# A perceiver block on one core: the tail after the cross attention, done batch by batch inside the loops

## The reference

```
x = x + xattn(layernorm(x), ctx, ctx)      # 16 heads, 2048 keys per batch
x = x + attn(layernorm(x))                 # 16 "heads" by a plain reshape, + its own layernorm
x = x + ffn(layernorm(x))                  # router argmax over 4 experts

# attn: Q = x@wq+bq ; K, V alike ; reshape(B*16, 128, 32) ; softmax(QK^T/sqrt(32)) V ; reshape back ; @wo + bo + x ; layernorm
# ffn:  logits = x @ W_router ; e = argmax(logits)
#       h = gelu(x @ W1[e] + b1[e])        # W1: 4 experts of 512 x 2048
#       y = layernorm(h @ Wo + bo + x)
```

## Time and profile before

| | us |
|---|---|
| median of 3 runs | 601.75 (601.21 to 604.71) |
| the profiled execution | 603.38 |
| its span, first to last instruction | 601.6 |
| PE busy | 528.6 (88%) |
| PE weight loads | 393.9 (65%) |
| DVE busy | 311.2 (52%) |
| ACT busy | 184.1 (31%) |
| POOL busy | 37.2 (6%) |
| mean granted TensorE clock | 0.933 of full |

### The profile page before, as it was taken

The page is one execution under the profiler, slowest core; times in us unless marked ns, Lnnn a source line. Parts: engine busy times, 40 slices in busy tenths (PEclk is TensorE's granted clock), DMA queues, the critical chain, the costliest instruction groups (busy, mean ns, idle before and its releaser), DMA issues.

```text
span 601.6 us, 8656 instructions
## 1 busy us (share of the span) xinstructions
PE 528.6 (88%) x3550; PEld 393.9 (65%) x3550; DVE 311.2 (52%) x561; ACT 184.1 (31%) x282; POOL 37.2 (6%) x32
## 2 busy tenths in 40 slices
PE   6999999999989899999999587934555999999995
PEld 5777767777767688777767455823225788888642
DVE  4545335566756411175757222874286579766122
ACT  3110053737363431136363720493222000000400
POOL 0300000003940000000000000000000000000000
PEclk9999999999989999999999798977765699999999
DMA  8600000004300000300004420000020565542000
GB/s 290 253 0 1 1 1 1 2 2 144 138 0 3 1 0 1 139 3 2 1 1 185 167 99 9 0 3 1 0 70 2 244 246 200 212 173 113 0 8 28
DMA packets 7998, 41.24 MB, mean 69 GB/s; under 512 B 1172, under 2 KB 2196, under 8 KB 4116
## 3 DMA queue, kind: packets, MB, share of 16 engines
q1 hardware_dynamic: 7960, 40.69, 18.3%
HBM read 40.16 MB, written 0.52 MB: 68 GB/s over the span
## 4 chain that ended last, share of the span: by engine, by line
PE 80%; DVE 9%; ACT 5%; issue 3%; DMA 1%; POOL 0%; SPq 0%; POOLq 0%; DVEq 0%; ACTq 0%
PE ps L778 41%; PE ps L835 10%; PE ps L821 6%; PE ps L1051 5%; PE ps L1052 5%; PE ps L1053 5%; PE ps L850 5%; ACT VT L396 2%; DMA wv_raw<-in_xWv 1%; PE ps L1040 1%; DVE rden L665 1%; DVE Pm L526 1%; DVE small L484 1%; DVE cT L672 1%; ACT Pm L325 1%
## 5 line engine op out<-in xcount | busy, mean ns | idle before, releaser
L333 ACT COPY PT<-ps 128x512 f32<-128x512 f32 x96 | 53.3, 588 | 102.0 <-PE ps L835 102.0
L835 PE MATMUL ps<-ident,Pm 128*128 128x128 f32 x512 | 71.1, 282 | 4.9 <-ACT PT L333 2.7
L835 PEld LDWEIGHTS ps<-ident,Pm 128*128 128x128 f32 x512 | 57.8, 143 | 24.9 <-issue 16.9
L526 DVE TENSOR_SCALAR_CACHE_REDUCE Pm<-ps,small 128x512 f32<-128x512 f32 x96 | 66.4, 748 | 8.6 <-PE ps L821 8.6
L325 ACT ACTIVATE Pm<-Pm,small 128x2048 f32<-128x2048 f32 x32 | 64.2, 2006 | 14.2 <-DVE Pm L526 14.2
L778 PE MATMUL ps<-ctxH,wkH 128*128 128x512 f32 x124 | 52.0, 419 | 2.8 <-DVE Kr L506 2.4
L1051 PE MATMUL ps<-w1H,zH 128*128 128x512 f32 x128 | 50.7, 396 | 0.0
L778 PE MATMUL ps<-wvH,ctxH 128*128 128x512 f32 x128 | 50.3, 393 | 0.2 <-DVE wvL L570 0.2
L1052 PE MATMUL ps<-w1L,zH 128*128 128x512 f32 x128 | 50.5, 395 | 0.0
L1053 PE MATMUL ps<-w1H,zL 128*128 128x512 f32 x128 | 50.3, 393 | 0.0
L778 PE MATMUL ps<-wvL,ctxH 128*128 128x512 f32 x128 | 50.0, 391 | 0.0
(11 more groups left out here) (151 smaller groups left out, 718.4 us busy)
## 6 DMA issues: line engine op xcount, KB each, us to landing
w1raw<-in_W SPq DMA_DIRECT2D x16, 1024.0 KB, 4.8
raw<-in_ctxT SPq DMA_DIRECT2D x7, 1024.0 KB, 4.9
woF<-in_ffn_Wo SPq DMA_DIRECT2D x1, 4096.0 KB, 14.0
rows<-in_rows SPq DMA_DIRECT2D x6, 256.0 KB, 3.9
raw<-in_ctxT SPq DMA_DIRECT2D x2, 512.0 KB, 6.2
wv_raw<-in_xWv SPq DMA_DIRECT2D x2, 512.0 KB, 8.5
wq<-in_xWq SPq DMA_DIRECT2D x1, 1024.0 KB, 12.9
wo<-in_xWo SPq DMA_DIRECT2D x1, 1024.0 KB, 4.7
```

What stands on the lines that cost most here:

```text
L333: act.copy(PT[:, c % 2, i, :, :].rearrange("p k t -> p (k t)"), ps[:, T_BANKS[i % 2], :]).then_inc(pt_act, 1)
L526: dve.tensor_scalar(Pm[:, i, c * CH:(c + 1) * CH], ps[:, i, :], -1.0, mx[:, p % 2, i, c - 1:c] if c else NOT_YET, ALU.mult, ALU.min, accum ...
L835: last = pe.transpose(ps[:, T_BANKS[i % 2], j * P:(j + 1) * P], Pm[:, i, c * CH + j * P:c * CH + (j + 1) * P], ident[:])
```

## The change

The tail is written for one batch at a time.

- **Batch 0's second attention** is placed among the 16 blocks of value products at the end of round 4: the cross attention's output product, layernorm, transposes, Q, K, V, scores, softmax, transposes and outputs, each step after one or two blocks. Its Q, K and V products have 128 moving columns in place of 256. DVE and ACT get its steps between the copies of V blocks. The four weights of this stretch come one after the other through one buffer `wS`, each loaded when the product before it is done.
- **Batch 0's steps up to the router and the masked tokens** are placed in rounds 5 to 8 (`alongside` on DVE; `attention2_out`, `normalized_T`, `logits`, `masks` on PE). They use PSUM bank 6, which is also the bank of the keys, so `keys` waits for them at two places (`u_done`, `x2T_done`), and all the cross attention's other banks stay as they were.
- **Batch 0's experts** are plain fp32 products of the raw W1 tiles (`first_experts`, 4 matmuls for a tile, no split), through a ring of four raw buffers; two tiles in round 8, the others between the steps of batch 1's chain, which runs after round 8 as the whole tail did before.
- **Batch 1's experts** are as before, in fp32r with split tiles, but the 16 tiles of W1 are loaded a second time, and the high part is made on ACT (L525), the low part on DVE (L916). Batch 0's gelu, transposes and the first two quarters of its output product are placed between tiles 1 and 2, after 7 and after 11.
- The biases of the experts are one plain fp32 matmul for each chunk instead of two in fp32r. The addition of the cross attention's output bias to x moves from round 7 to round 1.

The core of the diff, with lines left out:

```diff
             for p in range(1, NP + 1):
                 more = p < NP
                 late = p >= 2 and p != G + 1
+                if p == NP:
+                    onehots_T(0)
+                    first_experts(0)
                 if more:
+                    if p == G + 2:
+                        pe.wait_ge(u_done, 1)
+                    if p == G + 3:
+                        pe.wait_ge(x2T_done, 1)
                     keys(p, 0)
...
                 for c in range(C):
+                    if p == G + 1 and c == 3:
+                        attention2_out(0)
+                    if p == G + 2 and c == 3:
+                        normalized_T(0)
+                    if p == G + 3 and c == 3:
+                        masks(0)
                     probs_T(p - 1, c, 0)
                     probs_T(p - 1, c, 1)
                     if c == 0 and more:
                         keys(p, 2)
+                    if c == 0 and p == NP:
+                        first_experts(1)
...
                 if p == G:
                     weighted_values(p - 1, C - 1)
                     reciprocals_T(p - 1)
-                    for c in range(C):
-                        for j in range(JT):
-                            values(1, c, j)
+                    while_values(0)
+                    while_values(1)
+                    attention_out(0)
+                    while_values(2)
+                    while_values(3)
+                    tokens_T(0)
+                    while_values(4)
+                    features(0, 0)
+                    while_values(5)
+                    while_values(6)
+                    features(0, 1)
+                    while_values(7)
+                    while_values(8)
+                    features(0, 2)
+                    while_values(9)
+                    scores2(0)
+                    while_values(10)
+                    while_values(11)
+                    probs2_T(0, 0)
+                    probs2_T(0, 1)
+                    while_values(12)
...
+                    values2_T(0)
+                    while_values(14)
+                    outputs2(0)
+                    while_values(15)
...
+            def first_experts(n):
+                if n == 0:
+                    pe.wait_ge(s_done, NP * C * HPG)
+                pe.wait_ge(z0_done, n // KT + 1)
+                pe.wait_ge(w1_in[n % RING], 16 * (n // RING + 1))
+                for c in range(IC):
+                    last = pe.matmul(ps[:, c, :], z[:, n, :], w1raw[n % RING][:, c * CH:(c + 1) * CH],
+                                     start=(n == 0), stop=False)
+                last.then_inc(first_tile, 1)
...
+            for n in range(NW1):
+                k = NW1 + n
+                act.wait_ge(w1_in[k % RING], 16 * (k // RING + 1))
...
+                if n >= 2:
+                    act.wait_ge(w1_tile, n - 1)
+                act.copy(w1H[n % 2][:], w1raw[k % RING][:]).then_inc(w1_hi, 1)
...
+            for n in range(NW1):
+                dve.wait_ge(w1_hi, n + 1)
...
+                dve.tensor_tensor(w1L[n % 2][:], w1raw[(NW1 + n) % RING][:], w1H[n % 2][:].bitcast(F32),
+                                  ALU.subtract).then_inc(w1_split, 1)
```

More of the change, by code:

```diff
@@ L877, in _ @@
                 pe.wait_ge(norm_done, b + 1)
[L878 removed]
+                transposes([xn[:, b, k * P:(k + 1) * P] for k in range(KT)], b, xT_mm)
             pe.wait_ge(xT_done, B)
@@ new lines, in attention2_out, with normalized_T @@
+            def attention2_out(b):
+                pe.wait_ge(wS_in, 16 * 5)
+                pe.wait_ge(cT_dve[b], HPG * (2 if b else HPG))
+                if b:
+                    pe.wait_ge(cT_act[b], 2 * HPG)
+                else:
+                    pe.wait_ge(k_done, C * (G + 2))
+                product(ps[:, O2_BANKS[b], :], [(cT[b][:, k, :], wS[:, k, :]) for k in range(KT)]).then_inc(o2_mm, 1)
+            def normalized_T(b):
+                pe.wait_ge(norm_done, LN4[b] + 1)
+                if not b:
+                    pe.wait_ge(k_done, C * (G + 3))
+                transposes([y[b][:, k, :] for k in range(KT)], XT_BANKS[b], x2T_mm)
@@ new lines, in logits, with masks @@
+            def logits(b):
+                pe.wait_ge(wr_in, 16)
+                pe.wait_ge(x2T_done, b + 1)
+                if not b:
+                    pe.wait_ge(s_done, (G + 3) * C * HPG)
+                product(ps[:, LOGIT_BANKS[b], 2 * P:2 * P + E], [(yT[b][:, k, :], wr[:, k, :]) for k in range(KT)])\
+                    .then_inc(logit_mm, 1)
+            def masks(b):
+                pe.wait_ge(z_ready, b + 1)
+                if not b:
+                    pe.wait_ge(k_done, C * NP)
+                for e in range(E):
+                    last = pe.matmul(ps[:, MASK_BANKS[b], e * T:(e + 1) * T], onehot[:, b, e:e + 1].to_broadcast([P, P]),
+                                     ident[:], start=True, stop=True)
+                last.then_inc(mask_mm, 1)
@@ new lines, in hidden_T, with ffn_out @@
+            def hidden_T(b, c):
+                pe.wait_ge(gelu_done[b], c + 1)
+                transposes([hid[b][:, (4 * c + k) * P:(4 * c + k + 1) * P] for k in range(KT)], 4 * b + c, hT_mm[b])
+            def ffn_out(b, c):
+                pe.wait_ge(woF_in, 16 * KT)
+                if c == 0 and b:
+                    pe.wait_ge(hT_dve[0], 1)
+                pe.wait_ge(hT_dve[b] if c % 2 else hT_act[b], c // 2 + 1)
+                for k in range(KT * c, KT * (c + 1)):
+                    last = pe.matmul(ps[:, b, :], hidT[b][:, k, :], woF[:, k, :], start=(k == 0), stop=(k == IT - 1))
+                if c == KT - 1:
+                    last.then_inc(f_mm, 1)
@@ new lines, in _ @@
+            logits(1)
+            first_experts(14)
+            masks(1)
+            onehots_T(1)
+            first_experts(15)
+            expert_bias(0)
+            for n in range(NW1):
+                second_experts(n)
+                if n == 1:
+                    for c in range(KT):
+                        hidden_T(0, c)
+                if n in (7, 11):
+                    ffn_out(0, n // KT - 1)
+            expert_bias(1)
+            ffn_out(0, 2)
+            ffn_out(0, 3)
```

957 lines of the change are left out of this document (536 added, 421 removed).

## The result

| | before | after |
|---|---|---|
| median of 4 runs each, us | 602.56 (601.21 to 604.71) | 569.1 (567.0 to 569.39) |
| ratio | | 0.9434, 95% interval 0.9396 to 0.9472 |
| span of the profiled execution, us | 601.6 | 566.8 |
| mean granted clock | 0.933 | 0.975 |

The forecast was 567.0, so it missed by 2.1 us of 33.5.

A forecast was written before the change was run, and what follows sets the result against it. PE was taken as busy nearly throughout except in the tail's first 119 us, where steps wait and the clock is low. 387.7 + 82.6 + 61.0 + 33.4 = 564.7, plus 2 for the clock: span and time 567 us, range 556 to 583.

The forecast's parts named there:

- the low clock's allowance: Ahead of the experts, behind thin bias products: 2 us added to the sum for PE at low clock.
- Step 1: Value products: batch 0's second attention among the blocks makes the stage 65.6 us instead of 43.6, +22.0.
- the walk's narrow margins: Value products: wk and wv land half a microsecond before they are wanted; softmax's fourth piece at 52.3, wanted at 54.
- Step 2: Rounds 5 to 7: added PE work +6.0, a wait for u_done before round 6 +2.7, smaller terms; sum +7.9 us.
- Step 3: Round 8: two of batch 0's expert tiles go in and delay the exponentials; PE goes on 2.8 us later.
- Step 4: Batch 1's chain: batch 0's tiles cover its steps, 80.5 us of PE work plus gaps, 82.6 us instead of 118.4.
- Step 5: Batch 1's experts: a loop of ACT, DVE and PE over two buffer pairs, 3.6 us a tile, 61.0 us in all.
- Step 6: End: biases, output products, transposes and last layernorm take 33.4 us.
- (a): Value products and rounds: in-order queues bite, six steps by some 2 us, 579 us; chance 0.17.
- (b): Batch 1's experts run at the low clock because of 0.9 us holes per tile, 591 us; chance 0.07.
- (c): Behind round 8: W1 is read twice and DMAs set the pace, 664 us; chance 0.03.
- (d): 128-column products cost 0.221 us and batch 1's expert loop 3.3 us a tile, 559 us; chance 0.10.

The follow-up runs named there:

- e5: The changed kernel with three pairs of split buffers instead of two in batch 1's experts; 561.16 us, ratio 0.9306.
- e2: The changed kernel with batch 0's second attention placed behind the 16 value blocks instead of among them; 597.37 us.
- e6: The changed kernel with DVE's addition behind u_done moved ahead of step 5's last four score passes; 564.62 us, ratio 0.938.
- e7: The changed kernel with round 8 reordered: reciprocals' product before the first expert tile, fourth exponential earlier, masked tokens a round later; 564.5 us, ratio 0.9366.
- e1: The changed kernel with batch 0's expert tiles 2 to 15 moved behind batch 1's chain on PE; 611.75 us.
- e3: The changed kernel loading only 64 of 2048 columns of each tile in the second reading of W1, leaving work out; 567.31 us.
- e4: The changed kernel with batch 1's experts in plain fp32 too, without the split; 574.49 us, ratio 0.9536.
- e8: The changed kernel with the edits of e5, e6 and e7 together; 554.53 us, ratio 0.9202.
- e9: The changed kernel, two pairs kept, with batch 1's bias products one group each behind expert tiles 2 to 5; 564.81 us, ratio 0.9369.
- e10: The changed kernel with the edits of e5, e6, e7 and e9 together; 552.14 us, ratio 0.9155.

## Why the prediction was right, step by step

The mechanisms of all six steps were found in the traces. That the sum agrees to 0.1 us in the span (566.7 and 566.8) is luck, for errors cancel: rounds 5 to 7 and round 8 came 5.4 us longer together, and three terms (the value products, the chain, the low clock's allowance) 6.1 shorter. The 2 us for the low clock were put behind the biases, where this execution paid nothing, and none into the rounds, where it paid 5.7; in e5 the rounds paid 1.9 and the end 3.4.

**Step 1, value products: +20.5 for +22.0.** PE has no wait and a clock of 1.00 there, so the walk's narrow margins (wk, wv, the softmax) all held; e2 shows what they hide, 30 us. The term that was off is the 128-column fp32 product, taken at 0.256 us. The chain of waits of the kernel after gives it:

```profile
403.50 10.98 PE ps L942 x96
```

96 records are 48 products, 0.229 us each, near the lower bound of 0.221. "The weight load is what doesn't shrink" was the wrong choice: records stand 0.114 us apart there while each one's weight load is 0.192 us long in the trace, so the loads overlap and don't set the pace. All 96 products in the two chains make 2.6 us less than I had, 1.3 of the 1.5 us in this stage.

**Step 2, rounds 5 to 7: +10.2 for +7.9.** The wait at `u_done` came where it was forecast, 3.4 us against 2.7, and e6 shows both that it is DVE's order that makes it and what was left out: behind it, twelve matmuls at half clock, +2.5 us. These two are 3.2 us more than forecast, so the rest of these rounds came 0.9 below.

**Step 3, round 8: +5.9 for +2.8.** The same omission: a wait of 3.3 us, then a tile at 6.62 us for 3.43. e7 gets 4.9 of the 5.9 back by the order alone, so most of the price was that of the queue's order and the clock, not of the work put there.

**Step 4, batch 1's chain: 80.0 for 82.6.** PE's work of 80.5 us was the bound; 1.3 are again the 128-column products, the gaps came to 1.4 us (80.0 less 78.56 busy), not 2, and the last 0.7 are in the rest of PE's work. e1 shows the cover: without the tiles 69.7 us for the chain, with 30 us of it idle.

**Step 5, batch 1's experts: 61.5 for 61.0.** The mechanism is confirmed by e5: with a third pair 53.3. The parts: the cast measured 1907 ns, which answers to the extrapolated 1.97, the low part 2.29. Casts of the loop start alternately 3.4 and 4.1 us apart, that is 7.5 us for two tiles, where 7.2 was forecast: the hand-overs between engines take 0.5 to 0.6, not 0.2. The Trainium skill ("ScalarE: Activation LUTs", What ACT_TABLE_LOAD costs) had given an estimated 1.89 us for the cast, and the trace agrees with that formula to 1%. The groups of DVE and ACT in the expert stage, kernel after (busy and mean, then idle and who ended it):

```profile
L916 DVE TENSOR_TENSOR w1L<-w1raw,w1H 128x2048 fp32r<-128x2048 f32 x14 | 32.1, 2291 | 20.4 <-ACT w1H L525 20.4
L525 ACT CAST w1H<-w1raw 128x2048 fp32r<-128x2048 f32 x14 | 26.7, 1907 | 27.7 <-PE ps L1218 27.7
```

Read in a ring: DVE waits for ACT, ACT for PE, and PE, 6.9 us in all, for DVE. None is busy all the time, and that is the sign of too few buffers.

**Step 6, end: 33.7 for 33.4,** and the 2 us for the clock behind the biases did not come in the profiled execution of after (3.63 us of biases, then 7.08 for the output product). They came in other kernels: with the eight bias products right ahead, the 16 records took 7.08 to 7.13 us in after, e2 and e3, and 8.6 to 10.1 in e1 and e4 to e8.

**The rivals.** (a) was half there: two queues did bite, at 3.4 and 3.3 us, and with the clock each cost nearly twice its wait in this execution; the other margins held. (b) did not happen: waits of 0.4 to 1.8 us in the loop left the clock at 1.00 (window 471.6 to 533.2). The Trainium skill ("TensorE: Matmul & The Clock Gate", Why this matters for your kernels), which says that only longer idle gaps bring it down, agrees with this loop, and with the waits of 3.3 and 3.4 us in rounds 5 and 8, to which I had not applied it. It doesn't cover all that the traces show, and there the traces decide: behind bias products the clock fell with no such gap (e4), and ahead of the value stage it fell behind short ones. Kernel after, PE, at 172 us:

```profile
171.93 0.49 PE L1026 MATMUL ps<-ident,rexp 128*128 128x128 f32 x2 [1.85 <-DVE rexp L609]
...
173.77 0.63 PE L942 MATMUL ps<-ctxH,wkH 128*128 128x512 f32 x1
174.20 0.63 PE L942 MATMUL ps<-ctxH,wkL 128*128 128x512 f32 x1
```

The kernel before has the same there, behind a wait of 1.75 us, so "the trace agrees as far as it goes" in the prediction had overlooked a row. (c) is ruled out by e3. (d) was right on the 128-column products and wrong on the loop.

**What stays open.** Why the clock falls in the stretch behind the bias products in some kernels and not in others. With the biases elsewhere it stayed up at the end in both kernels that were run (e9, e10), against three of nine with them there. Behind the eight products ahead of the loop, which all these kernels have, it fell in five of eleven (e1, e4, e7, e8, e10; in e10 the products themselves took 4.54 us for 3.63). That the thin products are the cause is likely by this, not shown. Open is also why the same wait draws a long, a short or no stretch of low clock.

## What to carry to other kernels

A dependent chain costs what it leaves PE idle, and can cost again in clock; put independent matmuls between its steps before anything else, since without such work between the steps (e1) the kernel lost 9 us, and with it won 33. When work is threaded into in-order queues, look at each engine for the one instruction that another waits for and move it ahead of bulk work: two such moves (e6, e7) were worth 5.6 and 4.9 us in their stages against after's execution, of which 3.1 and 1.3 us were wait and 2.5 and 3.0 the clock behind it. Where three engines wait for each other in a ring and none is busy, add a buffer (e5, 8.2 us) before changing the arithmetic (e4, whose stage lost 3.9 us, some 2 without the low clock). And compare two kernels' profiled executions only after looking where the clock was down in each: it made differences of 2 to 3 us in stages with the same code.

## What the runs showed of the hardware that I had not expected

- A single wait of PE of 3.3 to 3.45 us, in the midst of dense work at full clock, was followed by matmuls at 1.2 GHz in 15 of 16 places (two in each of after, e1 to e5 and e9, one in e6 and e7), but not for equally long: the first tile of round 8 took 6.5 to 6.7 us in after, e2, e3, e6 and e9 and 5.1 to 5.4 in e1, e4 and e5, for 3.4 at full clock, and in e5 the keys of round 6 ran at full clock.
- Shorter waits can do it too. Behind one of 1.75 to 1.9 us at some 172 us the clock fell in nine of the twelve kernels, behind one of 2.19 us ahead of the value products in two (e4, e6), behind one of 2.0 us in round 8 in one of three with the same code there (5.37 us for the tile in e8, 3.67 in e7 and e10). Waits of up to 1.8 us in the expert loop of after were never followed by it.
- A plain fp32 product of 128 columns costs 0.229 us, a fourth of one of 512 (0.866) within 6%: it gets shorter with its columns down to there.
- 270 GB/s for 80 us, and 382 in the window from 395.0 to 403.5, ran beside PE, DVE and ACT with no wait of an engine put down to a DMA in the profile; the demand behind round 8 that the prediction feared is well inside what the DMAs gave.
